# Eight reordered steps in a one-core kernel of four graph and four feed-forward layers on Trainium2

## The chip, the cores and the metric

The kernel runs on one core of one Trainium2 chip. The metric is the device time of one launch in microseconds. Before the change it is 889.49 us (median of 3 runs, 886.07 to 890.65).

## The reference

384 nodes with 512 features pass through eight residual steps, a graph step and a feed-forward step in each of four layers. Each gets the layer-normalised x and adds its result to x:

```
x = x + _L0_gnn_ref(_layernorm(x), edge_index, ...)   # attention over 6144 edges, softmax over nodes, elu, norm
x = x + _L0_ffn_ref(_layernorm(x))                    # the "shifter", below
x = x + _L1_gnn_ref(_layernorm(x), edge_index, ...)   # three graph convolutions with relu and graph norm
x = x + _L1_ffn_ref(_layernorm(x), w_up, w_down)      # quantised linear pair
x = x + _L2_gnn_ref(_layernorm(x), edge_index, W, b)
x = x + _L2_ffn_ref(_layernorm(x), ...)               # six experts, top 1, gelu
x = x + _L3_gnn_ref(_layernorm(x), src, dst, deg, ...)# self and neighbour product, bias, norm
x = x + _L3_ffn_ref(_layernorm(x), ...)               # 64 experts, top 8 of 4 groups
```

The shifter reads flags and three one-hot digits out of its normalised input and adds two one-hot digits to it:

```
hot = x_bd > 0.5
lo, hi, sa = first16(64), first16(80), first16(96)     # first hot position of 16, else 0
val = lo + 16 * hi
shl, shr = (val << sa) & 255, val >> sa
res = shl if mark and is_shl, shr if mark and is_shr, else 0
out = x_bd with 2*active*one_hot(res & 15) added at 128:144 and 2*active*one_hot(res >> 4) at 144:160
```

The last step, for each token:

```
scores = sigmoid(x2 @ gate_w.T); s = scores + gate_b
# the 4 groups of 8 experts with the largest sum of their two best s; the 8 best s inside them
w = chosen scores / their sum * 2.5
y = sum over the 8 chosen experts e of w_e * (silu(x2 @ w1[e]) * (x2 @ w3[e])) @ w2[e]
```

## The kernel before

The 384 tokens are three tiles of 128 partitions (NT = 3), the features four chunks of 128 (KD = 4). Everything is written by hand for five queues: SP (all plain loads and stores), GpSimd (gathers and scatters by index), TensorE, ScalarE and VectorE. Each is one list of instructions, executed in order, and semaphores join them. On VectorE `go` issues an instruction that counts up one semaphore, `settle` waits for all of them, `one` does both; an instruction that reads another's result stands behind a `settle`.

A **norm** on VectorE (`layernorm`, `tile_root` and `tile_norm`) takes statistics of a tile, has ScalarE take the root (`row_root`), inverts it and writes the normalised tile. TensorE transposes it (`transposes`) and ScalarE copies the transposed tile out of PSUM (`copy_T`). ScalarE's order of roots and copies is written out.

**Layer 0.** Scores of the edges are scattered to a table in DRAM of 384 x 384 x 8. SP reads it back in three tiles of 1.5 MB (L315), VectorE finds each row's maximum in `row_max` by halving (L1326, L1328), subtracts it (L1333), TensorE transposes and multiplies. Meanwhile GpSimd quantises weights (L472 to L474).

**Shifter** (L1372 to L1431). VectorE normalises x into xn3 in full width, and releases GpSimd, which adds xn3 to x3 (L478). VectorE goes on with small instructions on xn3: three comparisons of 48 columns (L1376), a maximum, some 30 instructions on 3 to 9 columns, six one-hots (L1427). Then it waits for GpSimd's adds and adds 32 columns (L1430). The norm for layer 1 ("3") follows.

**L3 graph step** ("7" and "8" are the norms ahead of it and behind it). TensorE: transposes of tile 0, `own_part(0)`, transposes of tiles 1 and 2, the neighbour product over all tiles (L768), then own and neighbour parts, then the transposes of norm 8 and the router's logits. ScalarE: root and copy alternate for the tiles of norm 7; for each tile of norm 8 two roots and one copy.

**Router.** After the sigmoid VectorE ranks the groups, and per tile takes the eight best (L1627), their positions (L1628) and replaces them (L1629); two comparisons and casts give `picked`, TensorE counts it (L788, L790) and VectorE has each token's place in its expert (`place1`, L1637).

**Experts.** 64 experts with 64 slots each make 32 expert tiles of two; eight places for overfull experts make two more (NTILE = 34). Weights come in 1.5 MB pieces into NWB = 11 buffers, two for each tile; the load of expert e waits for the `down` product of the tile that used its buffer (L335). Tile 0's tokens are picked by a matmul with one-hots (`pick_first_tokens`, L816). For the others VectorE takes slot codes out of PSUM (`take_code` for tiles 1 and 2, `take_slots` later), and GpSimd gathers 128 token rows from `tok_tab` in DRAM (L492), which SP has stored (L350). The loop per tile i on TensorE: `transpose_tokens(i + 1)` (L824), `transpose_hidden(i - 1)`, `up(i)` (L835), `find_slots(i + 3)`, `down(i - 1)` (L855), `combine(i - 2)` (L863). `combine` multiplies a one-hot spread with the result in three bf16 parts: ScalarE writes the high part (L1068), VectorE what is left (L1681), ScalarE the middle part (L1070), VectorE the low part (L1683). After the loop VectorE adds the three banks to x3 (L1818) and SP stores.

## Time and profile before

| | us |
|---|---|
| median of 3 runs (lowest, highest) | 889.49 (886.07, 890.65) |
| profiled execution, its time | 888.59 |
| profiled execution, its span | 886.9 |
| busy: TensorE, VectorE, ScalarE, GpSimd | 640.7, 532.8, 277.4, 229.4 |
| mean granted TensorE clock | 0.831 |

The span is the time between first and last instruction on the chip; the metric adds what lies around it. Positions (start us) count from the span's start. Busy times of different engines overlap, and only a view that tells what each instruction waited for says which of them costs time.

### The profile page before, as it was taken

How to read it: one execution, taken by the hardware profiler on the slowest of the kernel's cores; microseconds unless marked ns; L12 is line 12 of the kernel's file. 1: busy time of each engine (PE TensorE's matmuls, PEld its weight loads, DVE VectorE, ACT ScalarE, POOL GpSimd, SP SyncE). 2: the span in 40 equal slices, each digit the busy share in tenths (PEclk: the TensorE clock that was granted, in tenths of full speed). 3: DMA queues.
4: the chain of work that ended last, by engine and by line, in shares of the span. 5: the costliest groups of instructions: out<-in, count | busy, mean ns of one | idle time of the engine just before them, and what ended most of it. 6: DMA issues, size and time to landing. Idle time of an engine off the chain costs nothing.

```text
span 886.9 us, 9573 instructions
## 1 busy us (share of the span) xinstructions
PE 640.7 (72%) x2855; PEld 311.0 (35%) x2878; DVE 532.8 (60%) x1472; ACT 277.4 (31%) x1103; POOL 229.4 (26%) x232
## 2 busy tenths in 40 slices
PE   5952424433234850998588998848999999999997
PEld 3420112111112750445335554433344344344332
DVE  3457988679697979444635225664447844445533
ACT  2104755456563330333504011111222222222222
POOL 5154776676772721000000000001011011111100
PEclk9985556665555965999598999969999999999999
DMA  8599486776875707900300000285999999999991
GB/s 337 229 384 320 132 260 214 237 245 190 276 211 202 249 1 257 383 1 8 135 0 1 0 1 0 80 326 203 405 418 412 406 395 408 419 408 417 417 364 38
DMA packets 46502, 208.08 MB, mean 235 GB/s; under 512 B 7953, under 2 KB 12561, under 8 KB 36848
## 3 DMA queue, kind: packets, MB, share of 16 engines
q1 hardware_dynamic: 27152, 145.70, 41.5%
q0 software_dynamic: 19296, 61.75, 20.9%
q8 instruction: 24, 0.39, 0.2%
q14 instruction: 30, 0.25, 0.1%
HBM read 199.67 MB, written 10.31 MB: 237 GB/s over the span
## 4 chain that ended last, share of the span: by engine, by line
PE 48%; DVE 6%; DMA 4%; ACT 1%; issue 1%; DVEq 0%; POOLq 0%; SPq 0%
PE bank L835 11%; PE bank L863 6%; PE bank L855 6%; PE bank L725 4%; PE bank L740 3%; DMA R<-tok_tab,slot_tok 3%; PE bank L646 3%; PE bank L539 2%; PE bank L640 2%; PE bank L824 2%; PE bank L534 1%; PE bank L747 1%; DMA R<-L_w 1%; PE bank L695 1%; PE bank L768 1%
## 5 line engine op out<-in xcount | busy, mean ns | idle before, releaser
L583 PE MATMUL bank<-R 128*128 128x384 bf16 x144 | 50.0, 483 | 141.1 <-DVE R L1258 106.7
L960 ACT ACTIVATE R<-R 128x128 f32<-128x128 f32 x384 | 113.3, 296 | 103.2 <-DVE R L1297 73.6
L835 PE MATMUL bank<-R 128*64 128x512 f32 (+1 forms) x432 | 106.6, 602 | 0.5 <-ACT R L1050 0.5
L492 POOL DMA_INDIRECT R<-tok_tab,slot_tok x33 | 33.2, 1006 | 269.6 <-DVE slot_f L1657 212.2
L539 PE MATMUL bank<-R,late 128*128 128x512 f32 x168 | 79.8, 635 | 0.0
L960 ACT ACTIVATION_READ_ACCUMULATOR R<-R 128x1 f32 x384 | 72.1, 188 | 14.7 <-issue 14.6
L583 PEld LDWEIGHTS bank<-R 128*128 128x128 bf16 x144 | 13.3, 119 | 173.1 <-DVE R L1258 125.5
L863 PE MATMUL bank<-R 128*128 128x512 bf16 x284 | 68.5, 380 | 3.6 <-issue 1.9
L1669 DVE TENSOR_TENSOR R<-R,bank 128x256 f32<-128x256 f32 x34 | 14.3, 420 | 90.9 <-ACT R L1062 90.9
L1293 DVE TENSOR_TENSOR R<-R 128x1032 f32<-128x1032 f32 x48 | 59.0, 1229 | 15.8 <-DMA R<-tab_dst,e_i 12.0
L450 POOL DMA_INDIRECT score<-late,e_i x48 | 57.4, 1196 | 42.4 <-DVE late L1252 25.4
L436 POOL DMA_INDIRECT R<-tab_src,e_i x48 | 50.5, 1053 | 39.2 <-DMA tab_src<-R 24.1
L1297 DVE SCALAR_TENSOR_TENSOR R<-R,sm 128x1024 f32<-128x1024 f32 x48 | 59.0, 1228 | 1.7
L855 PE MATMUL bank<-R 128*64 128x512 f32 (+1 forms) x216 | 55.5, 599 | 0.5 <-ACT R L1056 0.5
L443 POOL DMA_INDIRECT R<-tab_dst,e_i x48 | 49.3, 1028 | 22.2 <-issue 13.7
L481 POOL MEMSET R<- 128x512 f32 x3 | 1.6, 526 | 201.0 <-DVEq L1584 200.9
L534 PE MATMUL bank<-ident,late 128*128 128x128 f32 x72 | 15.0, 375 | 49.0 <-DVE late L1176 35.2
L539 PEld LDWEIGHTS bank<-R,late 128*128 128x128 f32 x168 | 34.9, 210 | 42.3 <-issue 41.8
L835 PEld LDWEIGHTS bank<-R 128*64 128x64 f32 (+1 forms) x432 | 30.3, 134 | 48.2 <-issue 47.7
L863 PEld LDWEIGHTS bank<-R 128*128 128x128 bf16 x306 | 27.2, 98 | 56.4 <-DVE R L1675 23.6
L1062 ACT ACTIVATE R<-bank 128x256 f32<-128x256 f32 x34 | 13.1, 385 | 107.9 <-PE bank L835 107.9
L835 PE MATMUL bank<-late,R 128*64 128x512 f32 (+1 forms) x144 | 43.8, 598 | 0.0
(371 smaller groups left out, 1163.4 us busy)
## 6 DMA issues: line engine op xcount, KB each, us to landing
R<-L_w SPq DMA_DIRECT2D x54, 1536.0 KB, 10.7
late<-L_w SPq DMA_DIRECT2D x18, 1536.0 KB, 9.6
R<-L_w SPq DMA_DIRECT2D x2, 3072.0 KB, 15.2
score<-R POOLq DMA_DIRECT2D x9, 512.0 KB, 11.8
R<-score SPq DMA_DIRECT2D x3, 1536.0 KB, 10.1
R<-L_Ww SPq DMA_DIRECT2D x2, 2048.0 KB, 12.5
R<-L_W SPq DMA_DIRECT2D x4, 1024.0 KB, 9.0
tab_src<-R SPq DMA_DIRECT2D x3, 516.0 KB, 3.0
```

What stands on the lines that cost most here:

```text
L436: pool.indirect_dma_start(out=ga[j], out_offset=None, in_=tab_src[:, :], in_offset=bass.IndirectOffsetOnAxis(ap=src_i[:, t:t + 1], axis=0) ...
L443: pool.indirect_dma_start(out=gd[j], out_offset=None, in_=tab_dst[:, :], in_offset=bass.IndirectOffsetOnAxis(ap=dst_i[:, t:t + 1], axis=0) ...
L450: pool.indirect_dma_start(out=score[:, :], out_offset=bass.IndirectOffsetOnAxis(ap=row_i[:, t:t + 1], axis=0), in_=w_e3[:, t, :], in_offse ...
L539: last = pe.matmul(pb[bank][:, cols_], lhsT[:, k, P * t:P * t + P], rhs[:, k, :], start=(k == chunks_[0]), stop=(k == chunks_[-1]))
L583: last = pe.matmul(pb[s][:, 0:N], oh[:, e % 2, 0, P * s:P * s + P], oh[:, e % 2, 1, :], start=(e == 0), stop=(e == ET - 1))
L725: last = pe.matmul(pb[j % 3][:, 0:N], F2W1[:, e, k, P * c:P * c + P], xT[:, k, :], start=(k == 0), stop=(k == KD - 1))
L835: last = pe.matmul(pb[4 + i % 2][part, :], xeT[i % 2][:, k, part], w13[e % NWB][:, k, :], start=(k == 0), stop=(k == KD - 1), tile_positio ...
L855: last = pe.matmul(pb[7][part, :], hT[i % 2][:, c, part], w2e[e % NWB][:, c, :], start=(c == 0), stop=(c == 1), tile_position=(0, part.start))
L863: last = pe.matmul(pb[t][:, :], spread[i % NSM][:, P * t:P * t + P], y_part[i % 2][c], start=(i == 0 and c == 0), stop=(i == NTILE - 1 and ...
L960: act_.activation(own, own, ACT.Copy, accum_out=w_e3[:, t, h:h + 1]).then_inc(S("heads_summed"), 1)
L1293: tt(ga[j], ga[j], gd[t % NGD], ALU.add).then_inc(S("rows_added"), 1)
L1297: stt(prod[t % 2].rearrange(heads, h=H), ga[j][:, 0:2 * D].rearrange(heads, h=H), 0.0, bc(waR[:, None, :], [P, H, P]), ALU.max, ALU.mult). ...
```

## The change

1. SP reads the first score tile back in two halves (by node column), and `row_max(0)` takes the maximum over the first half when it has landed and the second when all has. The order of the comparisons differs, the result doesn't.
2. SP stores the three token tiles ahead of the loads of experts 5, 6, 7 and 9, each as soon as it is normalised.
3. GpSimd no longer adds xn3 to x3. ScalarE writes x3 · (1 + rstd) − mean · rstd in place instead, from two small vectors that VectorE makes. The norm ahead of the shifter writes columns 0 to 111 only, and the shifter is rewritten in fewer instructions.
4. TensorE runs `up(1)` ahead of the transposes of tile 2's tokens and of tile 0's hidden rows; the later tiles keep their order.
5. ScalarE takes the roots of tiles 1 and 2 of norm 7 ahead of the copy of tile 1, and the first root of tile 1 ahead of the copy of tile 0 in norm 8.
6. Router: the three maxima, then the three replacements, then `picked` at once in bf16; the searches for positions move behind the weight split; the copy of the loads moves behind the one-hots of tile 2.
7. `take_code(1)` stands ahead of `onehots(2)`.
8. The last expert tile is combined part by part (high, middle, low), and VectorE adds each bank when its last product is done.

```diff
@@ SP
-            for i in range(NT):
+            own = score[0:N * P, :].rearrange("(p n) h -> p n h", p=P)
+            sp.dma_start(mt[0][:, 0:N // 2], own[:, 0:N // 2]).then_inc(S("half_back"), 16)
+            sp.dma_start(mt[0][:, N // 2:N], own[:, N // 2:N]).then_inc(S("read_back0"), 16)
+            for i in range(1, NT):
...
             load_expert(8)
+            for t in range(NT):
+                sp.wait_ge(S("xn_ready"), nth("8", t + 1))
+                own = tok_tab[0:2 * P, :].rearrange("(p c) d -> p c d", c=2)[:, 0, :] if t == 0 else tok_tab[P + P * t:2 * P + P * t, :]
+                sp.dma_start(own, xn3[:, t]).then_inc(S("tokens_stored"), 16)
             sp.wait_ge(S("x_ready"), NT * 7)
             for e in (5, 6, 7, 9):
                 load_expert(e)
-            for t in range(NT):
...
@@ GpSimd
-            pool.wait_ge(S("shifter_in_ready"), 1)
-            for t in range(NT):
-                pool.tensor_tensor(out=x3[:, t, :], in0=x3[:, t, :], in1=xn3[:, t, :], op=ALU.add).then_inc(S("shifter_added"), 1)
@@ TensorE
+            def combine_last():
+                i = NTILE - 1
+                pe.wait_ge(S("spread_ready"), NTILE)
+                for c, part in enumerate(("y_high_ready", "y_mid_ready", "y_low_ready")):
+                    pe.wait_ge(S(part), NTILE)
+                    for t in range(NT):
+                        last = pe.matmul(pb[t][:, :], spread[i % NSM][:, P * t:P * t + P], y_part[i % 2][c], start=False, stop=(c == 2), skip_group_check=True)
+                        if c == 2:
+                            last.then_inc(S("combined"), 1)
...
-            for i in range(1, NTILE + 2):
+            for i in range(1, NTILE + 1):
+                if i == 1:
+                    up(1)
                 if i + 1 < NTILE:
                     transpose_tokens(i + 1)
                 if 1 <= i <= NTILE:
                     transpose_hidden(i - 1)
-                if i < NTILE:
+                if 1 < i < NTILE:
                     up(i)
...
+            combine_last()
@@ ScalarE
+            act_.wait_ge(S("shifter_in_ready"), 1)
+            for t in range(NT):
+                act_.activation(x3[:, t, :], x3[:, t, :], ACT.Identity, scale=V_("rstd_1", 3)[:, t:t + 1], bias=V_("nmr", 3)[:, t:t + 1]).then_inc(S("shifter_added"), 1)
...
+            row_root(0)
+            copy_T("7", 0)
+            row_root(1)
+            row_root(2)
+            copy_T("7", 1)
+            copy_T("7", 2)
+            row_root(0)
+            row_root(0)
+            row_root(1)
+            copy_T("8", 0)
+            row_root(1)
+            copy_T("8", 1)
+            row_root(2)
+            row_root(2)
+            copy_T("8", 2)
@@ VectorE, row_max
+                if i == 0:
+                    dve.wait_ge(S("half_back"), 16)
+                    go(tt(half_max[:, 0:768], mtf[i][:, 0:768], mtf[i][:, 768:1536], ALU.max))
+                    dve.wait_ge(S("read_back0"), 16)
+                    one(tt(half_max[:, 768:1536], mtf[i][:, 1536:2304], mtf[i][:, 2304:3072], ALU.max))
@@ VectorE, shifter
+            layernorm(x3, xn3, produce=add_norm(yr), produced=x_tile_ready(0), part=slice(0, 112))
+            go(stt(first, xn3[:, :, 64:112], 0.5, bc(fall48[:, None, :], [P, NT, 48]), ALU.is_gt, ALU.mult))
+            go(ts(mark, xn3[:, :, 0], 0.5, None, ALU.is_gt))
+            go(ts(flags[:, :, 1:3], xn3[:, :, 39:41], 0.5, None, ALU.is_gt))
+            go(ts(V_("rstd_1", 3), rstd, 1.0, None, ALU.add))
+            settle()
+            go(dve.tensor_reduce(far, V_("first", 144).rearrange("p (c i) -> p c i", i=16), AX, ALU.max))
+            stt(V_("nmr", 3), mv[:, :, 0], -1.0, rstd, ALU.mult, ALU.mult).then_inc(S("shifter_in_ready"), 1)
+            go(tt(both, shl, shr, ALU.mult))
+            settle()
...
+            one(tt(ones2, bc(iota64[:, None, None, 0:16], [P, NT, 2, 16]), bc(nibs[:, :, :, None], [P, NT, 2, 16]), ALU.is_equal))
+            go(tt(first[:, :, 0:32], first[:, :, 0:32], bc(amp[:, :, None], [P, NT, 32]), ALU.mult))
             settle()
             dve.wait_ge(S("shifter_added"), NT)
@@ VectorE, router
-                v8 = top8[:, 8 * t:8 * t + 8]
-                one(dve.max(v8, masked[:, t, :]))
-                go(dve.max_index(smi[:, 8 * t:8 * t + 8], v8, masked[:, t, :]))
-                go(dve.match_replace(replaced[:, t, :], v8, masked[:, t, :], NEG))
-            settle()
-            go(dve.tensor_copy(idx8f, smi[:, 0:24]))
+                go(dve.max(top8[:, 8 * t:8 * t + 8], masked[:, t, :]))
+            settle()
+            for t in range(NT):
+                go(dve.match_replace(replaced[:, t, :], top8[:, 8 * t:8 * t + 8], masked[:, t, :], NEG))
+            settle()
+            ts(WK[:, 1536:1632].bitcast(bf16), WK[:, 896:1088], -2e38, None, ALU.is_lt).then_inc(S("picked_ready"), 1)
             go(ts(WK[:, 1088:1280], WK[:, 896:1088], -2e38, None, ALU.is_lt))
-            settle()
-            dve.tensor_copy(WK[:, 1536:1632].bitcast(bf16), WK[:, 1088:1280]).then_inc(S("picked_ready"), 1)
...
-            dve.tensor_copy(load_s[:, :], pb[7][:, E3 * NT:E3 * NT + E3]).then_inc(S("place_used"), 1)
-            dve.wait_ge(S("place_used"), 1)
...
+            take_code(1)
             onehots(2)
-            take_code(1)
+            dve.tensor_copy(load_s[:, :], pb[7][:, E3 * NT:E3 * NT + E3]).then_inc(S("place_used"), 1)
+            dve.wait_ge(S("place_used"), 1)
@@ VectorE, end
-            dve.wait_ge(S("combined"), NTILE)
             for t in range(NT):
+                dve.wait_ge(S("combined"), NTILE + t)
                 tt(x3[:, t, :], x3[:, t, :], pb[t][:, :], ALU.add).then_inc(S("x_ready"), 1)
```

## Rows read from the trace of the kernel before

**Rows 1.** The page's chain that ended last, shares by engine:

```profile
PE 48%; DVE 6%; DMA 4%; ACT 1%; issue 1%; DVEq 0%; POOLq 0%; SPq 0%
```

**Rows 2.** Stretches: length, busy by engine, granted clock, DMA share, GB/s:

```profile
606.00:608.00 2.00, 2.00 (x8) 0.89 (x8) 1.33 (x7) 0.38 (x1) 1.01 (x1) 0.50 0.00 0
632.00:880.00 248.00, 243.47 (x1375) 96.28 (x1391) 127.06 (x450) 63.75 (x122) 27.00 (x27) 1.00 0.93 382
```

**Rows 3.** Landings of L315; timeline (start, length, engine, line, [idle before]):

```profile
DMA to landing us min/median/max: 6.7/10.1/13.3
...
284.82 1.76 DVE L1326 TENSOR_TENSOR R<-R 128x1536 f32<-128x1536 f32 x1 [2.48 <-DMA R<-score]
```

**Rows 4.** Timeline of the shifter; ScalarE's scaled Identity of the next layer:

```profile
339.52 1.13 DVE L1176 TENSOR_SCALAR late<-x_s,sm 128x512 f32<-128x512 f32 x2
340.69 2.64 DVE L1376 SCALAR_TENSOR_TENSOR sm<-late,fall 128x48 f32<-128x48 f32 x3
340.78 3.70 POOL L478 TENSOR_TENSOR x_s<-x_s,late 128x512 f32<-128x512 f32 x3 [25.51 <-DVEq L1373]
...
343.70 0.81 DVE L1380 TENSOR_SCALAR sm<-sm 128x9 f32<-128x9 f32 x1
...
345.04 0.16 DVE L1391 TENSOR_SCALAR sm<-late 128x3 f32<-128x3 f32 x1
...
349.41 0.26 DVE L1430 TENSOR_TENSOR x_s<-x_s,sm 128x96 f32<-128x96 f32 x1
...
422.28 0.81 ACT L1000 ACTIVATE late<-late,sm 128x512 f32<-128x512 f32 x1 [0.61 <-DVE sm L1473]
```

**Rows 5.** Timeline of the L3 graph step, VectorE and TensorE:

```profile
544.43 0.17 DVE L1196 RECIPROCAL sm<-sm 128x1 f32<-128x1 f32 x1 [2.40 <-ACT sm L934]
...
545.23 0.66 PE L534 MATMUL bank<-ident,late 128*128 128x128 f32 x4 [1.63 <-DVE late L1197]
...
568.55 0.16 DVE L1597 RECIPROCAL sm<-sm 128x1 f32<-128x1 f32 x1 [0.37 <-ACT sm L934]
```

**Rows 6.** Timeline of the router, VectorE, and the pick on TensorE:

```profile
585.49 0.23 DVE L1627 MAX8 sm<-R 128x8 f32<-128x64 f32 x1
...
587.95 0.26 DVE L1634 CAST R<-R 128x192 bf16<-128x192 f32 x1
...
589.36 0.23 DVE L1639 COPY load_s<-bank 128x64 f32<-128x64 f32 x1
...
591.62 4.34 PE L816 MATMUL bank<-R,late 128*128 128x128 f32 x24 [0.64 <-DVE R L1734]
```

**Rows 7.** Timeline of stores, gathers, token transposes; landings of all 33 gathers:

```profile
577.08 1.52 SPq L350 DMA_DIRECT2D tok_tab<-late  x3
...
597.26 1.12 POOL L492 DMA_INDIRECT R<-tok_tab,slot_tok  x1 [50.21 <-DVE slot_f L1729]
...
603.71 0.66 PE L824 MATMUL bank<-ident,R 128*128 128x128 f32 x4 [3.15 <-DMA R<-tok_tab,slot_tok]
...
621.50 0.66 PE L824 MATMUL bank<-ident,R 128*128 128x128 f32 x4 [0.29 <-DMA R<-tok_tab,slot_tok]
...
628.03 1.00 POOL L492 DMA_INDIRECT R<-tok_tab,slot_tok  x1 [7.64 <-DVE slot_f L1657]
...
637.80 0.60 PE L824 MATMUL bank<-ident,R 128*128 128x128 f32 x4
...
DMA to landing us min/median/max: 4.3/8.1/9.7
```

**Rows 8.** Chain (start, length, what) of the last load; timeline of the end:

```profile
856.97 8.07 DMA R<-L_w
...
867.19 3.57 PE bank L835 x32
...
877.08 2.12 PE L863 MATMUL bank<-R 128*128 128x512 bf16 x9
...
882.36 1.88 DVE L1818 TENSOR_TENSOR x_s<-x_s,bank 128x512 f32<-128x512 f32 x3 [2.29 <-PE bank L863]
```

94 lines of the change are left out of this document (40 added, 54 removed).

## The prediction

> **What bounds the kernel now.** I read four views in this order: the chain that ended last, the engine shares by stretch, the timelines of the edited stretches, and the landings of DMAs. The chain gives 48% of the span to TensorE, 6% to VectorE and 4% to DMA [rows 1]: no engine binds throughout, and each edit must be priced in its own stretch. In the expert loop (632 to 880) TensorE works 243.5 of 248 us at the full clock while the DMA share is 0.93 [rows 2]; so a saving ahead of the loop moves it as a whole, and nothing in it gets shorter. From 606 to 608 the granted clock is 0.50, the lower of its two levels (1.2 against 2.4 GHz) [rows 2], just behind a wait of TensorE for gathered tokens. In the stretches ahead of the loop the chain runs through VectorE (softmax, shifter, router) or passes back and forth between it and TensorE, and there a saved wait is a saved microsecond.
>
> All positions below are those of the profiled execution of before: its time is 888.59 us, its span 886.9, so 1.7 us lie around the span and stay. Its median is 889.49.
>
> **1. First read of the scores in halves.** VectorE waits 2.48 us for the read, then takes 1.76 us for the first maximum over 1536 columns [rows 3]. The three equal reads land 6.7, 10.1 and 13.3 us after issue, so one of them flows for some 3.6 us, and its first half lands 1.8 us ahead of the whole, at about 283.0, when VectorE has been free since 282.3. Half of 1.76 is 0.88; it runs in the wait, and the path keeps 0.9 us after the whole has landed. Gain 1.76 − 0.9 = 0.85, less the second issue on SP (0.33 to 0.43, mostly under the flow): **0.8**, bounds 0.3 and 0.9. The reads behind it come 0.4 later, and the second isn't wanted before the first has been worked on for some 9 us, 5 us after it lands. VectorE has no gap from here to 316, so all of it carries on.
>
> **2. Shifter and short norm.** The last normalised tile ends at 340.65, and the shifter's last add (349.41 + 0.26) lets the next norm begin at 349.71 [rows 4]. Of these 9.06 us, 2.64 go to three comparisons of 48 columns at 0.93 each and 0.81 to one instruction on nine columns; both lie inside GpSimd's three adds (340.78 to 344.48). Later instructions of that size take 0.16. After the change the adds are on ScalarE. The new VectorE chain has 16 links. Rows give 0.16 for a tiny instruction, 0.07 for each one behind it in its link, 0.04 to settle, 0.26 for 96 columns, so about 0.30 for 144 [rows 4]: 0.56 + 0.49 (comparison, then maximum) + 0.27 + 0.34 + 5 × 0.27 + 2 × 0.20 + 2 × 0.27 + 0.29 + 0.30 + 0.30 = 4.84, against 9.06: 4.2 less. ScalarE starts about 1.0 us into it; the nearest row is the scaled Identity in place on 128x512, 0.81 [rows 4], so three take 2.4 and end 1.4 us ahead of the VectorE chain. They are hidden; with a table load of 1.28 they still would be, and that same row shows Identity behind Sqrt without one. The norm with 112 columns in place of 512: 0.53 and 1.13 become three of about 0.2, and the end is then set by ScalarE's last root: 1.1 us earlier. Together 5.3, taken as **5.2**, bounds 3.8 (links at 0.30) and 5.6. What comes next: TensorE waits for norm 3, whose layer-1 weights are issued at 337.3 and wanted at 355.3; 5.2 sooner still leaves 12.8 us for transfers of the 9.0 us kind.
>
> The Trainium skill ("SBUF — State Buffer", "Who interferes with whom") says that a VectorE instruction with two SBUF inputs and a GpSimd instruction that reads SBUF block each other fully; the trace agrees with 0.93 us beside the adds where 96 columns later take 0.26.
>
> **3. L3 order on ScalarE.** The root of tile 2 stands behind the copy of transposed tile 1, which waits for TensorE; VectorE waits 2.40 and TensorE then 1.63 us for the last transposes, with the neighbour product behind them [rows 5]. With both roots ahead of that copy, tile 2 is normalised at 543.0, TensorE goes from 543.6 straight on: **1.6**. The copy is wanted only 10 us later. In the second norm VectorE waits 0.37 for a root behind a copy [rows 5]; that goes, and TensorE's product for the next tile is then due about 0.1 short of it: **0.3**. Bounds for both 1.2 and 2.1. The third tile's order has no wait to lose.
>
> **4. Router chain.** From the first MAX8 at 585.49 to TensorE at 588.27 each of three tiles runs maximum, index search and replacement in 0.66, then casts (the last at 587.95) [rows 6]. Now: three maxima 0.51, three replacements 0.62, one comparison that writes bf16 0.25, settling 0.1: 1.5 against 2.73, so 1.25 less. The copy of the loads (0.23 and its settling, 0.26) leaves the path between place and one-hots as well. Together **1.5**: one-hots at 588.1, the pick of tile 0's tokens at 590.1, its end 594.4 (4.34 as today [rows 6]), first up product 595.1 to 598.6, slots of tiles 0 to 2 done at 599.05. The index searches (3 × 0.22 + 0.25, about 0.9) now stand before the copy of the first one-hots at 598.1: it lands around 598.0 in the new order, 0.6 ahead of TensorE. Cover gone, they would cost 0.9.
>
> **5. Token stores and second tile.** Today the three stores are issued behind four expert loads of 1.5 MB; the first gather starts at 597.26 and TensorE stands 3.15 us until 603.71 [rows 7]. On SP the stores now come first, at 565.9, 571.5 and 577.1; the four loads slip from 574.8 to 577.6 and end near 596, wanted from 608 on. The gather then waits for the codes, which moved ahead of the second one-hots: 590.2, plus 0.8 from release to DMA as today, so 591.0. It now flies beside the loads. Today's, with one load beside it, took 6.4 us (597.26 to 603.7); of all 33 the median is 8.1 and the longest 9.7 [rows 7]; I take 8.1, since the loads run to 596: 599.1, just as TensorE is free. So the transposes of tile 1 move from 603.71 to 599.1, 4.6 earlier. Then up(1) waits only for the copy of these transposes (0.7), starts at 600.6 instead of 606.75, and takes 3.6 at full clock or 4.36 as today. Its cost: the hidden transposes of tile 0 now come right before its down product, whose copy on ScalarE (0.38) is no longer covered: +0.5. down(0) ends at 607.3 to 608.1 (today 612.9), tile 4's transposes come one period of 8.1 later, at 615.4 to 616.2, or at 615.6 by their gather (607.5 + 8.1), against 621.50 today with its wait of 0.29 [rows 7]. Gain from the router's start to here 5.3 to 5.9, which includes the 1.5 of part 4; I take **5.4**. Lower bound 3.0: gather at 9.7 (−1.6) and a further late one (−0.8). Behind it SP's stream of 61 loads starts with down(0), so it moves with the loop.
>
> The skill's "SBUF — State Buffer" ("SBUF: two separate sides") speaks against this part: a DMA issued by GpSimd can't get its descriptors written while VectorE copies in a two-port mode, and it gives 3.1 us in place of 0.62. The first gather would now be issued in the middle of VectorE's one-hots and copies. The trace disagrees so far: beside the weight splits the two first issues took at most 1.12 us against 1.00 [rows 7]. By the rule the sum would be 2.5 us longer, 876.2.
>
> **6. Last combine in parts.** Today nine products wait for the last low part, which ends at 880.1, and VectorE waits 2.29 us for them before its three adds, 1.88 [rows 8]. Nine take 2.12 [rows 8], so 0.21 each and 0.4 for a single one. Now the first three run once the high part is there, at 879.2 behind combine(32), three more up to 880.5 at the latest, and of the last three the first is complete at about 880.75, with adds starting per tile as they run (0.6 apart). First add 880.75 instead of 882.36: **1.6**. Bounds 1.0 (VectorE's own branch after its last split could hold it) and 1.7. Last store and its landing stay.
>
> **Sum.** 0.8 + 5.2 + 1.6 + 0.3 + 5.4 + 1.6 = 14.9; 888.6 − 14.9 = **873.7 us**. All lower bounds: 0.3 + 3.8 + 1.2 + 3.0 + 1.0 = 9.3, so 879.3; all upper: 0.9 + 5.6 + 2.1 + 5.9 + 1.7 = 16.2, so 872.4. The two other runs of before lie 2.5 below and 2.1 above this execution, and I leave that much outside.
>
> **Rivals.** (a) The DMA stream takes over at the end. The last expert load lands at 865.05 [rows 8], and the product that needs it starts at 867.2: only 2.1 us of air. If the first gather or the early loads hold the stream's start while TensorE gains, what exceeds 2.1 is lost: of part 5's 5.4 about 3 remain, 876.1. For it: DMA share 0.93 over the loop. Against: the stream is released by the same down(0) that I move. (b) Blocked descriptors or slower gathers at the start: 876 to 878, by part 5's lower bound. (c) Slower than before: each tile's gather has only 9.8 − 8.1 = 1.7 us of air (issue 628.03, transposes 637.80 [rows 7]). If the denser start left the queue so full that gathers took over 10.3 us, every one of some 28 tiles would wait 0.5 us or more, which eats the 14.9; at 10.5 us, 0.7 × 28 − 14.9 = 5 us slower, 893. Against: of 33 gathers none takes over 9.7, and the median in a loop with a full queue is 8.1 [rows 7]. (d) The shifter shrinks less, since VectorE's 0.93 is its own and not GpSimd's: the one comparison of 144 columns then keeps up to 1.8 of the 2.64 and the nine columns 0.6, 876.1.
>
> **Chances.** Forecast (871.5 to 876) 0.60; (a), (b), (d) together, or several parts at their lower bounds (876 to 880), 0.22; better than summed (868.5 to 871.5) 0.10; nothing or little of it visible (880 to 893.9) 0.05; (c) 0.03. Range 869.5 to 880, which takes in the low ends and one run-to-run step below. A measurement of this kernel can tell 0.5%, 4.4 us, from no change. Over 0.5% faster 0.94, within 0.03, slower 0.03.
>
> **What would show it.** First maximum split with its first half inside the wait; from the last normalised tile to the next statistics 4.8 us, no instruction on nine columns over 0.3; no wait of VectorE for a root at 544; TensorE's counts 1.25 us sooner after the first MAX8; first gather issued before the pick ends, with TensorE waiting under 1 us for it, and a clock that doesn't fall to 0.5 behind it; the loop's period still 8.12; the last add 1.6 us nearer to the last split. A wait for a gather in every tile, or one for the last expert load, would make the prediction wrong.

## The result and the profile after

| | before | after |
|---|---|---|
| median of 4 runs, us | 887.78 | 876.93 |
| lowest, highest | 885.52, 890.65 | 867.93, 880.2 |
| profiled execution, its time | 888.59 | 867.93 |
| profiled execution, its span | 886.9 | 866.1 |
| busy: TensorE, VectorE, ScalarE, GpSimd | 640.7, 532.8, 277.4, 229.4 | 638.3, 527.4, 278.5, 227.4 |

The ratio after to before is 0.986, 95% interval 0.9816 to 0.9905: 12.4 us less, between 8 and 16. The forecast was 873.7 with a range of 869.5 to 880. Two things must be kept apart from the start. The profiled execution of after is the fastest of its four runs, 20.7 us below the profiled one of before, and only some 13 of these belong to the change; and the sum of the forecast was 14.9, so it was also a little too high. Both are taken apart below.

After, the page's chain by engine (against [rows 1]):

```profile
PE 58%; DVE 21%; issue 8%; ACT 6%; DMA 4%; POOL 2%; another core or an unknown queue 1%; DVEq 0%; SPq 0%; POOLq 0%
```

The two lines can't be compared: the shares of before add up to 60%, because its chain is followed back only to 348.5 us, near the end of the shifter, while that of after reaches back to the start. So the 48% and 6% from which the prediction started say nothing on the softmax and next to nothing on the shifter. Its prices don't rest on them.

After, two stretches, with length, busy by engine, granted clock, DMA share, GB/s (against [rows 2]):

```profile
586.00:588.00 2.00, 2.00 (x10) 0.67 (x12) 1.48 (x11) 0.00 (x0) 0.64 (x1) 1.00 0.03 11
612.00:858.00 246.00, 242.31 (x1369) 95.72 (x1386) 125.77 (x449) 63.15 (x121) 26.95 (x27) 1.00 0.94 383
```

The second up product (586 to 588 lies in it) now runs at the full clock, where in before it ran at 0.50. The loop is as full as before, TensorE 242.3 of 246 us; nothing in it got shorter.

After, timelines (start, length, engine, line, [idle before]) of the first maximum and of norm and shifter (against [rows 3, 4]):

```profile
280.17 0.96 DVE L1351 TENSOR_TENSOR R<-R 128x768 f32<-128x768 f32 x1 [0.40 <-DMA R<-score]
282.06 0.96 DVE L1353 TENSOR_TENSOR R<-R 128x768 f32<-128x768 f32 x1 [0.93 <-DMA R<-score]
...
331.62 0.32 DVE L1200 TENSOR_SCALAR late<-x_s,sm 128x112 f32<-128x112 f32 x1
...
331.98 0.71 DVE L1200 TENSOR_SCALAR late<-x_s,sm 128x112 f32<-128x112 f32 x2
332.72 0.31 DVE L1407 SCALAR_TENSOR_TENSOR sm<-late,fall 128x144 f32<-128x144 f32 x1
...
333.69 2.22 ACT L987 ACTIVATE x_s<-x_s,sm 128x512 f32<-128x512 f32 x3 [2.05 <-DVE sm L1414]
...
337.31 0.26 DVE L1458 TENSOR_TENSOR x_s<-x_s,sm 128x96 f32<-128x96 f32 x1
```

The first half of the maximum runs in the wait for the second. ScalarE's three adds end at 335.91, 1.4 us ahead of the last add of VectorE, as reckoned. But a write of 112 columns takes 0.32, not 0.2.

After, timelines of the third layer's graph step, the router and the first tiles (against [rows 5 to 7]):

```profile
528.49 0.16 DVE L1220 RECIPROCAL sm<-sm 128x1 f32<-128x1 f32 x1 [0.34 <-ACT sm L947]
...
529.12 1.04 PE L534 MATMUL bank<-ident,late 128*128 128x128 f32 x8
...
570.05 0.48 DVE L1654 MAX8 sm<-R 128x8 f32<-128x64 f32 x3
...
571.59 0.23 PE L788 MATMUL bank<-R,trib 128*128 128x64 bf16 x1 [6.84 <-DVE R L1659]
...
575.59 1.12 POOL L492 DMA_INDIRECT R<-tok_tab,slot_tok  x1 [44.48 <-DVE slot_f L1753]
```

```profile
574.68 5.25 PE L816 MATMUL bank<-R,late 128*128 128x128 f32 x24 [0.64 <-DVE R L1758]
...
584.46 0.66 PE L824 MATMUL bank<-ident,R 128*128 128x128 f32 x4
...
585.90 3.65 PE L835 MATMUL bank<-R 128*64 128x512 f32 x16 [0.54 <-DVE R L1687]
...
590.92 0.27 PE L803 MATMUL bank<-tok_w,R 128*64 128x4 bf16 x6 [0.56 <-ACT R L1080]
...
601.10 0.60 PE L824 MATMUL bank<-ident,R 128*128 128x128 f32 x4
```

The waits of 2.40 and 1.63 us of the third layer are gone (0.34 is the plain path of a root). The counts come 1.54 us behind the first MAX8, where it was 2.78. The first gather is issued before the pick ends; TensorE takes its tokens at 584.46 with no wait, where it stood for 3.15 us. The price named beforehand is there too: 0.56 us behind the hidden transposes.

After, timeline of the end (against [rows 8]):

```profile
858.99 2.10 PE L864 MATMUL bank<-R 128*128 128x512 bf16 x9
...
860.85 1.88 DVE L1848 TENSOR_TENSOR x_s<-x_s,bank 128x512 f32<-128x512 f32 x3 [0.82 <-PE bank L864]
861.56 2.27 SPq L376 DMA_DIRECT2D out<-x_s  x3
```

The adds start 0.82 us after VectorE's last split, where it was 2.29. The last row was not expected: the issues of the three output stores stretch over 2.27 us.

**One view of all.** Stretches between fixed points, from the starts and lengths in the timelines of each profiled execution. "Others like before" are experiments in which the code of that stretch is that of before; the next column has three executions of the changed kernel (the second and third are experiments 1 and 9).

| stretch, us | before | others like before | after, three times |
|---|---|---|---|
| score read issued to first maximum's end | 8.52 | 8.29 to 8.72 | 7.52, 7.41, 7.42 |
| to the last scaled softmax tile | 40.62 | 36.87 to 40.64 | 36.86, 37.90, 36.85 |
| to the last write of the norm | 13.45 | 13.44, 13.45 | 12.81, 12.81, 12.81 |
| to the shifter's last add | 9.02 | 9.02, 9.03 | 4.88, 4.90, 4.88 |
| to layer 2's last graph add | 114.65 | 114.72 to 116.48 | 115.24, 116.17, 114.77 |
| layer 2: last graph add to gate logits | 11.49 | 11.47 to 11.69 | 9.14, 11.72, 11.50 |
| gate logits to layer 3's norm done | 69.49 | 69.48 to 69.49 | 67.42, 67.43, 67.42 |
| to the router's start | 35.35 | 35.35 | 35.85, 35.86, 35.84 |
| to the first MAX8 | 4.83 | 4.83, 4.84 | 4.83, 4.83, 4.83 |
| first MAX8 to the counts | 2.77 | 2.77 | 1.54, 1.54, 1.54 |
| counts to the transposes of the fourth tile | 33.23 | 33.29 to 33.83 | 29.50, 28.54, 29.74 |
| these to the last split | 258.57 | 257.44 to 258.95 | 258.92, 258.37, 257.60 |
| last split to the last add's end | 4.17 | 4.17 | 2.71, 2.71, 2.70 |
| last add's end to the span's end | 2.62 | 2.61, 2.62, 2.62 | 3.39, 3.86, 4.09 |

Seven of these stretches repeat to 0.02 us. The others don't: the first maximum, the softmax, the layers between shifter and layer 2, the middle of layer 2, the way to the fourth tile, the expert loop and the end of the changed kernel; nor do the 275 to 282 us ahead of the score read. In the profiled pair three of them fell the same way, 2.6 us before the score read, 3.8 in the softmax and 2.3 in layer 2, together 8.7, with nothing of the change in their code; 0.9 fell the other way (0.6 behind the shifter, 0.35 in the loop). The edited stretches make up the remaining 13.

**A stretch that may take something back.** From the shifter's last add to layer 2's last graph add no instruction was edited. It takes 114.65 to 114.81 in the four executions with GpSimd's adds (before, experiments 3, 5 and 6), and 114.54 to 116.48 in the nine with ScalarE's adds and no additional work ahead of norm 3 (all others but experiment 12), in the mean 0.9 more. More than half of that (0.55) is the first product behind norm 3, here in before:

```profile
355.28 10.65 PE L539 MATMUL bank<-R,late 128*128 128x512 f32 x24
```

In experiment 2 the same 24 instructions start at 346.82 and take 11.76. In before the granted clock is 1.00 from 356 on, 0.7 us behind the product's start; in experiment 2 it is still 0.50 from 347 to 349, up to 2.2 us behind it. Three of the nine are as short as before, so the earlier shifter doesn't lengthen the stretch every time. Whether it does so more often, or six of nine against none of four is chance, no run settles.

### The profile page after: what moved, and what is told of

Same layout as the page of the kernel before. It is cut to its first block, busy times and chain, and to the rows that moved or that the text cites. A ratio compares the mean times of both kernels' runs of the same rounds, so it can differ in the third digit from the quotient of the medians.

```text
span 866.1 us, 9566 instructions
## 1 busy us (share of the span) xinstructions
PE 638.3 (74%) x2855; PEld 309.7 (36%) x2878; DVE 527.4 (61%) x1465; ACT 278.5 (32%) x1106; POOL 227.4 (26%) x229
## 4 chain that ended last, share of the span: by engine, by line
PE 58%; DVE 21%; issue 8%; ACT 6%; DMA 4%; POOL 2%; another core or an unknown queue 1%; DVEq 0%; SPq 0%; POOLq 0%
PE bank L835 13%; PE bank L539 7%; PE bank L873 7%; PE bank L855 6%; ACT R L973 4%; PE bank L725 4%; PE bank L740 4%; DVE R L1317 3%; DVE R L1321 3%; PE bank L646 3%; PE bank L640 2%; PE bank L824 2%; PE bank L534 2%; PE bank L747 1%; PE bank L752 1%
## 5 line engine op out<-in xcount | busy, mean ns | idle before, releaser
L873 PE MATMUL bank<-R 128*128 128x512 bf16 x275 | 66.4, 380 | 2.6 <-issue 2.1
L835 PEld LDWEIGHTS bank<-R 128*64 128x64 f32 (+1 forms) x432 | 30.1, 133 | 47.9 <-issue 46.7
## 6 DMA issues: line engine op xcount, KB each, us to landing
R<-L_Ww SPq DMA_DIRECT2D x2, 2048.0 KB, 12.4
```

Of the source, the lines that this page charges most:

```text
L835: last = pe.matmul(pb[4 + i % 2][part, :], xeT[i % 2][:, k, part], w13[e % NWB][:, k, :], start=(k == 0), stop=(k == KD - 1), tile_positio ...
L873: last = pe.matmul(pb[t][:, :], spread[i % NSM][:, P * t:P * t + P], y_part[i % 2][c], start=(i == 0 and c == 0), stop=False, skip_group_c ...
```

## The experiments

The theory: the gains are local, each about as priced, they add up, and nothing behind them takes them back. The rivals are named in each expectation. "Part" is a part of the prediction (1 to 6), not a number of the list of changes. Experiments 1 to 4, 5 to 8, 9 to 11 and 12 ran on four chips, each group beside runs of before on its own chip, with medians of before of 887.71, 872.24, 874.56 and 886.2. So only ratios are compared across groups.

**1, 9. The changed kernel again**, with no edit.

> The changed kernel once more, nothing altered, to see which of the stretches of its first profiled execution belong to the change. Theory (the gains are local, as priced): the stretches that the change touches come out again within 0.3 us: last norm store to the shifter's last add about 4.9, score read's issue to the first maximum's end about 7.5, third router maximum to the third tile's transposition about 31, last split to the last add 2.7; those that it does not touch and that differed (last maxima to the softmax's end 35.0, against 38.8 before; second layer's middle 7.2, against 9.5 before; edge stage 275.5, against 278.1 before) may come out at either length, following TensorE's granted clock. Median near 876. Rival (the change itself moved the softmax and the second layer): these stretches are short again, 35 and 7.2, in this execution too, with the clock high in the last softmax tile, and before's are long again.

> The changed kernel a third time, as the measure for the next two on one chip, and as a third look at the stretches that vary. Theory: ratio to the kernel before 0.986 again; score read to first maximum 7.4 to 7.5, shifter 4.9, third layer's stretch 67.4, first MAX8 to the transposes of tile 3 30 to 31, last add to end 3.4 to 4.1. The softmax stretch (36.9 to 40.7 in ten executions of all kernels) and the second layer's middle (9.1 once, 11.5 to 11.7 else) follow TensorE's clock, not the kernel. Rival: the change's gain is smaller than 1.4% and the first two measurements were lucky: ratio 0.990 or more.

Measured: ratios 0.9864 (0.9815 to 0.9913; 876.49 us) and 0.9867 (0.9823 to 0.9911; 862.29 us). Three measurements agree, 0.986, 0.9864 and 0.9867: 1.36%, 12 us. The table shows the rest: the stretches that the change touches came out again, and softmax and layer 2 went back to longer values in one or both, so they aren't the change's.

**2. Part 2 alone.** Before, with ScalarE's adds, the short norm and the new chain:

```
-            pool.wait_ge(S("shifter_in_ready"), 1)
-            for t in range(NT):
-                pool.tensor_tensor(out=x3[:, t, :], in0=x3[:, t, :], in1=xn3[:, t, :], op=ALU.add)...
+            act_.wait_ge(S("shifter_in_ready"), 1)
+            for t in range(NT):
+                act_.activation(x3[:, t, :], x3[:, t, :], ACT.Identity, scale=V_("rstd_1", 3)[:, t:t + 1], ...
...
-            layernorm(x3, xn3, produce=add_norm(yr), produced=x_tile_ready(0))
+            layernorm(x3, xn3, produce=add_norm(yr), produced=x_tile_ready(0), part=slice(0, 112))
```

> The kernel before with part 2 of the change alone: ScalarE's adds in place of GpSimd's, the shorter write in the norm, the rewritten shifter. Theory (each gain is local and they add up): about 4.8 us less than the kernel before (shifter 9.06 to 4.9, norm 1.70 to 1.07), ratio 0.9945. Rival (an earlier start of what follows runs against a later wait or a lower clock): under 3 us, with the shifter's own stretch still at 4.9. Rival (the shifter's saving also frees the second layer's middle, since the stages after it meet a warmer TensorE): 7 us or more, second layer's middle at 7.2.

Measured: 0.9935 (0.9904 to 0.9966), 882.66 us, 5.1 less by medians. Norm 12.81, shifter 4.88, as in the changed kernel. Layer 2's middle is 11.69, so the second rival is out. The first isn't: the layers between took 116.48, 1.8 more than in before, and the medians' difference, 5.1 ± 2.8, fits 4.8 and also 3.

**3. The start of the expert loop alone.** Before, with the router's chain, the token stores ahead, the second up product ahead, `take_code(1)` ahead:

```
+            for t in range(NT):
+                sp.wait_ge(S("xn_ready"), nth("8", t + 1))
+                ...
+                sp.dma_start(own, xn3[:, t]).then_inc(S("tokens_stored"), 16)
             sp.wait_ge(S("x_ready"), NT * 7)
             for e in (5, 6, 7, 9):
                 load_expert(e)
...
+                if i == 1:
+                    up(1)
                 if i + 1 < NTILE:
                     transpose_tokens(i + 1)
```

> The kernel before with the router's shorter chain, the token stores ahead of the four weight loads, the second tile's expert ahead of the third tile's transpositions and the hot code taken earlier. Theory: third maximum to third tile's transposition falls from 36.0 to about 31, and the kernel by 5 us, ratio 0.9945. Rival (the loop's steady course gives part of it back, because the weights arrive later behind the token stores or the gathers stay late): the stretch falls by 5 but the kernel by under 3 us. Rival (the saving depends on the warm clock that the third-layer order brought): first tiles at a lower clock again, stretch at 33 to 34, kernel 2 to 3 us less.

Measured: 0.9926 (0.9895 to 0.9958), 880.87 us, 6.8 less by medians. First MAX8 to the fourth tile's transposes 30.99, where it was 36.01, without the third layer's new order. The 5 us arrive at the end: from there to the last split it takes 258.44, as before.

**4. Who held VectorE in the shifter?** Before, with GpSimd's three adds given to ScalarE; VectorE's old chain and the long norm stay:

```
-                pool.tensor_tensor(out=x3[:, t, :], in0=x3[:, t, :], in1=xn3[:, t, :], op=ALU.add)...
+                act_.activation(x3[:, t, :], x3[:, t, :], ACT.Identity, scale=V_("rstd_1", 3)[:, t:t + 1], ...
```

> The kernel before with only GpSimd's three shifter adds replaced by three of ScalarE; VectorE's old chain of the shifter, the long norm and the rest stay. It settles whether the first comparisons of the shifter (0.93 us each beside GpSimd's adds) were long by themselves. Theory (they were held up by GpSimd's adds, which run in the same time): the three comparisons and the reduction after them fall to about 0.2 to 0.35 us each, the shifter from 9.06 to 6.5 to 7.5 us, the kernel by about 2 us. Rival (VectorE's own time): the comparisons stay at 0.93 us each and the stretch at 8.5 or more.

Timeline of experiment 4 (against [rows 4]):

```profile
337.41 0.44 DVE L1377 SCALAR_TENSOR_TENSOR sm<-late,fall 128x48 f32<-128x48 f32 x3
337.53 2.22 ACT L971 ACTIVATE x_s<-x_s,sm 128x512 f32<-128x512 f32 x3 [2.10 <-DVE sm L1374]
...
338.22 0.17 DVE L1381 TENSOR_SCALAR sm<-sm 128x9 f32<-128x9 f32 x1
```

The same three comparisons take 0.44 where they took 2.64, the instruction on nine columns 0.17 where it took 0.81, and the shifter 6.45 where it took 9.02. So 2.57 of the 4.14 us come from the adds' change of engine, though it has two small instructions more in its chain (0.4), and 1.57 from the shorter chain. Rival (d) is out: the 0.93 us were GpSimd's. The time, 885.51 us, ratio 0.9988 (0.9956 to 1.0019), is compatible with 2.6 us and with nothing (here too the layers behind took 116.23).

**5. The other three parts.** Before, with the halves of the score read, the new order of the third layer and the last combine by parts:

```
-            for t in range(NT):
-                row_root(t)
-                copy_T("7", t)
+            row_root(0)
+            copy_T("7", 0)
+            row_root(1)
+            row_root(2)
+            copy_T("7", 1)
+            copy_T("7", 2)
...
+            sp.dma_start(mt[0][:, 0:N // 2], own[:, 0:N // 2]).then_inc(S("half_back"), 16)
+            sp.dma_start(mt[0][:, N // 2:N], own[:, N // 2:N]).then_inc(S("read_back0"), 16)
...
+            combine_last()
```

> The kernel before with the three parts that neither of the two part kernels had: the first score read in halves, the order of roots and copies of the third layer on ScalarE, the last combine by parts. Theory (local gains): score read's issue to the first maximum's end 8.6 to 7.5, the third layer's stretch up to the router 1.6 shorter, last split to last add 4.2 to 2.7, but up to 1.2 of the last given back behind the last add; together 2.9 to 4.0 us less than before, which with 5.8 and 6.6 us of the two other part kernels makes up the whole change's 12 only if these two medians are some 3 us too good. Rival (the three parts are worth nothing on the path, the two others make up the whole): under 1 us less, with these stretches as before. Rival (a further loss from the earlier start): slower than the sum by over 1 us, seen as a longer loop.

Measured: 0.9957 (0.9927 to 0.9986), 868.89 against 872.24 us, 3.4 less by medians. First maximum 7.36, layer 3's norm 67.42, last add's end 2.70 behind the last split, all as in the changed kernel, and the end 4.08 behind it. Experiments 2, 3 and 5 together are 1.8% (0.65, 0.74, 0.43, each ± 0.3), the whole change is 1.4 ± 0.3% by its three ratios: no contradiction, and no proof that they add to the tenth either. In the edited stretches the part kernels and the whole change have the same lengths.

**6. The last combine alone:**

```
+            def combine_last():
+                ...
+                for c, part in enumerate(("y_high_ready", "y_mid_ready", "y_low_ready")):
+                    pe.wait_ge(S(part), NTILE)
+                    for t in range(NT):
+                        last = pe.matmul(pb[t][:, :], spread[i % NSM][:, P * t:P * t + P], y_part[i % 2][c], ...
...
-            for i in range(1, NTILE + 2):
+            for i in range(1, NTILE + 1):
...
+            combine_last()
...
-            dve.wait_ge(S("combined"), NTILE)
             for t in range(NT):
+                dve.wait_ge(S("combined"), NTILE + t)
```

> The kernel before with the last combine by parts alone. Two executions of the changed kernel had 3.4 and 3.9 us from the last add's end to the end, all executions without this part 2.6, because the issue of the second output store took 1.2 and 1.7 us on SP in place of 0.34. Theory (the earlier stores run into the two instruction fetches that come a fixed time behind the last split): the second issue is again over 1 us here, last add to end 3.4 to 3.9, net gain of the part 0.3 to 0.7 us. Rival (it is the queue's position, moved by the additional score read): the issue is 0.34 here, last add to end 2.6, net gain 1.45 us.

SP's output stores: the timelines of before and of experiment 6 (start, from the first issue to the end of the last):

```profile
883.07 1.53 SPq L373 DMA_DIRECT2D out<-x_s  x3
```

```profile
867.17 2.79 SPq L373 DMA_DIRECT2D out<-x_s  x3
```

Measured: 1.0001 (0.9974 to 1.0027). The last add ends 1.47 us nearer to the last split, and the end comes 3.90 us behind it in place of 2.62: 1.3 of 1.5 us are given back. It is the trace that tells this; the ratio, ± 2.3 us, can't. The position of the stores on their queue isn't the cause, since the additional score read is absent here.

**10. Is it SP?** The changed kernel with the second store on ScalarE's queue:

```
-            for t in range(NT):
+            for t in (0, 2):
                 sp.wait_ge(S("x_ready"), NT * 7 + t + 1)
...
+            act_.wait_ge(S("x_ready"), NT * 7 + 2)
+            act_.dma_start(out[P:2 * P, :], x3[:, 1]).then_inc(S("half_back"), 16)
```

> The changed kernel with the second output store issued by ScalarE, which has long been idle, in place of SP. In five executions of kernels with the last combine by parts one of SP's three store issues took 1.2 to 1.7 us in place of 0.34, and last add to end 3.4 to 4.1 in place of 2.6. Theory (SP's own issue is held, by its queue or an instruction fetch): with only two stores on SP, and ScalarE's beside them, last add to end is 2.6 to 3.0, 0.8 to 1.2 us less than the changed kernel. Rival (the DMA engines or their rings are held, whoever issues): one of the issues is long again and the end comes 3.4 us or more behind the last add; no gain.

Measured: 0.9852 (0.9808 to 0.9896), not to be told from the changed kernel. Every issue is short or nearly so (0.35, 0.37 and 0.60), and still the end is 3.38 behind the last add. Experiment 9 has all three issues short and its end is the latest of all, 4.09. So no issue is long, as the rival's sign had it, but its core holds: a second issuing queue gains nothing, so the issuing queue isn't what is held. What the packets in the traces show, in us from the last add's end (the output's packets belong to q1, the 16 KB one to q8, which the page calls instruction):

```
                 16 KB instruction packet   last output packet ends   span's end
before                     -1.99                     1.89                2.62
experiment 2               -1.99                     1.88                2.61
experiment 3               -1.93                     1.89                2.62
after                      -0.66                     2.65                3.39
experiment 1               -0.67                     3.13                3.86
experiment 6               -0.64                     3.16                3.90
experiment 9               +0.03                     3.28                4.09
experiment 10              -0.68                     2.57                3.38
```

The fetch comes 2.0 to 2.7 us behind the last split in all of them. In before that is 0.8 us ahead of the first store; with the combine by parts the stores have come forward into it, and their packets all but stop, from 0.5 to 1.0 in after and to 1.5 us in experiments 1 and 6, or straggle one by one in experiment 9. That the two stand together in all eight is measured, and the other six executions agree: the end comes 2.61 or 2.62 behind the last add in the four without the combine by parts, 3.37 to 4.09 in the ten with it. In seven of these ten SP issues all three stores and the 16 KB packet starts 0.64 to 0.70 ahead of the last add's end. There a longer such packet goes with a later end of the output: 2.65 and 2.63 for 0.93 and 1.02 us, 2.92 and 2.93 for 1.21, 3.05 for 1.36, 3.13 and 3.16 for 1.41 and 1.43. That the fetch holds the packets is still inferred; no run took the fetch away.

**7. Token stores back behind the loads.** The changed kernel with

```
-            for t in range(NT):
-                ...
-                sp.dma_start(own, xn3[:, t]).then_inc(S("tokens_stored"), 16)
             sp.wait_ge(S("x_ready"), NT * 7)
             for e in (5, 6, 7, 9):
                 load_expert(e)
+            for t in range(NT):
+                ...
+                sp.dma_start(own, xn3[:, t]).then_inc(S("tokens_stored"), 16)
```

> The changed kernel with one part undone: the three token stores again behind the loads of four experts. Theory (the first gather waits for these stores, as before): the first gather is issued again some 11 to 12 us behind the first of the last three MAX8 in place of 5.5, the transposes of tile 1 come 18 us behind it in place of 14.4 with TensorE waiting 3 to 4 us and its clock at 0.5 after that, and the kernel is 3.5 to 4.5 us slower than the changed one (about 880.5). Rival (the codes set the first gather, the stores have long landed): under 0.5 us slower. Rival (the four loads gain by going first): faster than the changed kernel.

Timelines of experiment 7:

```profile
576.11 1.11 POOL L492 DMA_INDIRECT R<-tok_tab,slot_tok  x1 [50.28 <-DVE slot_f L1753]
```

```profile
582.29 1.10 PE L824 MATMUL bank<-ident,R 128*128 128x128 f32 x4 [2.78 <-DMA R<-tok_tab,slot_tok]
...
584.17 6.12 PE L835 MATMUL bank<-R 128*64 128x512 f32 x16 [0.53 <-DVE R L1687]
```

The first gather is issued 11.3 us behind the first MAX8 (564.78) in place of 5.5, TensorE waits 2.78, and its clock falls: the second up product takes 6.12 where it takes 3.65. First MAX8 to the fourth tile 37.2, against 30.1 to 31.3: 6 to 7 us in this execution, and longer even than before's 36.0 to 36.6. The time says less: 865.78 us, 0.9909 (0.9877 to 0.9941), against 0.9864 for the changed kernel (mean of its three ratios), 3.9 us slower with some 4 either way.

**8. Second up product back.** The changed kernel with

```
-                if i == 1:
-                    up(1)
...
-                if 1 < i < NTILE:
+                if i < NTILE:
                     up(i)
```

> The changed kernel with one part undone: the up product of tile 1 again behind the transposes of tile 2 and the hidden ones of tile 0. Theory: the transposes of tile 2 must wait for the second gather, which comes some 2 to 4 us behind the first, so TensorE stands before them, the up product starts 2 to 4 us later, the transposes of tile 4 come at 32 to 34 us behind the first MAX8 in place of 30 to 31, and the kernel is 1.5 to 3 us slower. Rival (the second gather is there at once): the order is worth only what the hidden transposes' wait costs, the stretch is 29.5 to 30.5, so the old order would be as good or 0.5 us better.

Timeline of experiment 8:

```profile
578.28 0.71 PE L824 MATMUL bank<-ident,R 128*128 128x128 f32 x4 [1.45 <-DMA R<-tok_tab,slot_tok]
578.78 0.63 PE L844 MATMUL bank<-ident,R 128*128 128x128 f32 x2
579.34 5.03 PE L835 MATMUL bank<-R 128*64 128x512 f32 x16
```

TensorE waits 1.45 for the second gather, then runs the up product partly cold (5.03), and the fourth tile comes 33.8 behind the first MAX8, 2.6 to 3.8 later than in the changed kernel, as the theory said. The time, 0.9858 (0.9807 to 0.9908) from four runs, doesn't show it; its interval of ± 4.4 us can't.

**11. Does the clock make the two varying stretches?** The changed kernel with work that nobody reads, in TensorE's waits:

```
+            def keep_warm(n):
+                for _ in range(n):
+                    pe.transpose(pb[7][:, 0:P], ident[:, :], ident[:, :])
...
+                    if i == NT - 1 and c == 0:
+                        pe.wait_ge(S("half_sc_ready"), 1)
+                        keep_warm(10)
                     transpose_scores(i, c)
...
+            keep_warm(26)
             for t in range(NT):
                 if t == 0:
                     pe.wait_ge(S("x_ready"), NT * 4 + NT)
```

> The changed kernel with 36 additional transposes of the identity into a bank that nobody reads: 10 ahead of the last softmax tile's transpositions, 26 in the 3.9 us in which TensorE waits for the second layer's norm. Nothing else changes. Theory (the two stretches are long where TensorE's clock has fallen in the wait ahead of them): the second layer's middle falls from 11.5 to about 9.2, the softmax stretch stays at 36.9 to 38, with no 40.6 to 40.7, and the kernel is 2 to 4 us faster than the changed one. Rival (the clock falls all the same, since its level was decided before these stretches): the middle stays at 11.5 or more, the kernel is the same or up to 1 us slower by the additional work.

Layer 2's middle without the additional work (experiment 9), then with it (experiment 11):

```profile
445.45 2.79 PE L534 MATMUL bank<-ident,late 128*128 128x128 f32 x12 [3.88 <-DVE late L1200]
448.18 3.88 PE L708 MATMUL bank<-late,wg_s 128*6 128x128 f32 x24
```

```profile
442.97 3.00 PE L622 MATMUL bank<-ident 128*128 128x128 f32 x26
447.02 1.54 PE L534 MATMUL bank<-ident,late 128*128 128x128 f32 x12 [1.04 <-DVE late L1208]
448.48 2.79 PE L716 MATMUL bank<-late,wg_s 128*6 128x128 f32 x24
```

And the granted clock there (windows; the clock is the third number from the end), experiment 9, then 11:

```profile
446.00:450.00 4.00, 4.00 (x20) 2.99 (x19) 3.44 (x12) 2.06 (x6) 0.00 (x0) 0.50 0.00 0
```

```profile
447.00:451.00 4.00, 3.98 (x36) 3.27 (x36) 3.88 (x13) 2.12 (x6) 0.00 (x0) 1.00 0.02 4
```

At 0.50 (1.2 GHz), reached in the wait of 3.88 us, the twelve transposes take 2.79; at 1.00 (2.4 GHz), held with 3 us of additional work in that wait, 1.54. The wait alone doesn't decide it: in the profiled execution of after, TensorE waits the same 3.88 us with no additional work, the clock stays at 1.00, and the transposes take 1.54. Measured: 855.6 us, ratio 0.9775 (0.9733 to 0.9816), against 0.9867 for the changed kernel on the same chip. That is faster than both kernels. The stretch fell from 11.50 to 9.14. That explains 2.4 of the 6.7 us between the two medians; the profiled softmax, 36.85 in both, explains nothing, and the rest is within the intervals.

**12. More of it:** experiment 11 with 57 more transposes, 30 ahead of norm 3's, 22 during the router's grouping, 5 behind the counts.

```
+            pe.wait_ge(S("shifter_in_ready"), 1)
+            keep_warm(30)
...
+            pe.wait_ge(S("sigmoid_ready"), 1)
+            keep_warm(22, 6)
             pe.wait_ge(S("picked_ready"), 1)
...
+            keep_warm(5, 6)
```

> The kernel with the 36 additional transposes, and 57 more: 30 in the wait ahead of norm 3's transposes (from the shifter's input on), 22 while VectorE works on the router's groups, 5 behind the counts. Theory (stretches that begin cold behind a long wait of TensorE can be warmed in that wait): the first transposes of norm 3 take 1.5 us in place of 2.8, the product behind them starts at the full clock, so that the graph layers' stretch is 1.5 to 2.5 us shorter than its 69.4; the pick of tile 0's tokens falls from 5.3 to 3 to 4.5 us, of which at most 1 us reaches the transposes of tile 3, since the first gather comes then. Ratio to the kernel before 0.973 to 0.976. Rival (the clock falls again soon behind the additional work, or has not risen when it ends): these stretches as before, ratio 0.9775 to 0.979. Rival (the additional work itself gets in the way, being cold it takes 0.22 to 0.24 each): slower than 0.9775 with TensorE still in it when its inputs are ready.

Timeline of experiment 12:

```profile
339.11 5.98 PE L622 MATMUL bank<-ident 128*128 128x128 f32 x30 [16.20 <-DVE sm L1427]
345.97 1.63 PE L534 MATMUL bank<-ident,late 128*128 128x128 f32 x12 [0.88 <-DVE late L1213]
...
578.00 5.40 PE L828 MATMUL bank<-R,late 128*128 128x128 f32 x24 [0.64 <-DVE R L1771]
```

Measured: 869.89 us, 0.9804 (0.978 to 0.9828). Norm 3's transposes took 1.63 us and the graph layers 68.1 in place of 69.3 to 70.5; layer 2's middle was 9.14 again. The pick stayed cold, 5.40, with 27 transposes ahead of it: the clock was 1.00 from 574 to 576 and had fallen again before the pick began at 578. There the first rival holds. And the softmax was 40.73 long although its last tile ran at the full clock: this time the tile before it was cold, so the ten transposes ahead of the last tile are no cure. The ratio missed the 0.973 to 0.976 that the theory named; experiments 11 and 12 can't be told apart by their ratios.

## Why the prediction held, and where it didn't

The result is faster, as forecast, and inside the range, but not in the part of it that was given 0.60 (871.5 to 876). The median of after, 876.93, lies in the next one (876 to 880, 0.22), which was meant for rivals (a), (b) and (d) or several parts at their lower bounds. None of these came; what lacks is mostly part 6. Mean of the three executions of after against the mean of all like before, part by part:

| part | predicted | measured | how it came |
|---|---|---|---|
| 1 halves | 0.8 (0.3 to 0.9) | 1.1 (8.56 to 7.45) | right, above the bound |
| 2 shifter | 4.2 | 4.1 | right, its split too (experiment 4) |
| 2 short norm | 1.1 | 0.64 | mechanism right, mis-sized |
| 3 layer 3's order | 1.9 (1.2 to 2.1) | 1.6 (2.07 − 0.50) | right, a third term missing |
| 4, 5 router to fourth tile | 5.4 (3.0 to 5.9) | 5.5 (1.23 + 4.22) | right |
| 6 last combine | 1.6 (1.0 to 1.7) | 0.3 (1.47 − 1.16) | step "last store and its landing stay" wrong |
| sum (part 2 was taken as 5.2) | 14.9 | 13.2 | |

The measured sum fits the measured ratios, 12.1 us ± 2.3. With the unedited layers behind the shifter, 0.7 us longer in these three executions than in the four with GpSimd's adds, it would be 12.5; whether that belongs to the change is open, as said above.

**Part 1.** Of its 1.1, 0.80 is the shorter instruction behind the landing (1.76 to 0.96), as reckoned. The rest is that the second half is worked on 6.6 us after the first issue (282.06 − 275.49), where the whole was in before 6.8 and, in four other executions, between 0.2 sooner and 0.2 later; I had reckoned 0.1 of loss there.

**Part 2.** The term that was mis-sized is the row for 112 columns: "about 0.2" each, against 0.32 alone and 0.71 for two. So the last write is behind ScalarE's last root by its own length and the stretch gains 0.64. The shifter is 4.88 against 4.84 reckoned. By the Trainium skill ("SBUF — State Buffer", "Who interferes with whom") a VectorE instruction with two SBUF inputs and a GpSimd instruction that reads SBUF shut each other out for a whole instruction; experiment 4 agrees, 2.64 to 0.44 us for the three comparisons, which have two. The instruction on nine columns has one input and still fell from 0.81 to 0.17; the same section of the Trainium skill counts scalings like it among those that can take the shared ports in a two-port mode.

**Part 3.** The wait at 544 went and brought 1.85: the norm is done 2.07 sooner, and the product behind it starts 0.22 further behind, because the transposes of two tiles now run ahead of it (529.12, 1.04 for 0.66). The second wait of 0.37 went, a wait of 0.21 for TensorE's product came, and 0.2 is left of the 0.3. What no step had is a third term: the last transposes ahead of the router now fall on the lower clock. The timelines of before, then of after:

```profile
576.91 0.63 PE L534 MATMUL bank<-ident,late 128*128 128x128 f32 x4 [2.60 <-DVE late L1197]
```

```profile
561.01 1.09 PE L534 MATMUL bank<-ident,late 128*128 128x128 f32 x4 [2.42 <-DVE late L1221]
```

That is 0.46 of loss, 1.6 in all, and it isn't chance: the stretch from the first neighbour product's scaling to the router is 32.80 in every execution with the old order and 33.07 to 33.09 in every one with the new.

**Parts 4 and 5** are the core of the forecast. The first gather was put 5.5 us behind the first MAX8 (591.0 − 585.49) and came at 5.54; TensorE doesn't wait for it, the clock is 1.00 at the second up product, the hidden transposes cost 0.56 (0.5). That the sum came out to 0.1 is in part luck. The gather landed 5.1 us behind its issue (4.6 in experiments 1 and 9), where 8.1 had been taken; this gained nothing, since TensorE was busy for 3.8 us more (3.3 and 4.5). The pick was cold, 5.25 and 5.49 for 4.34 in two of the three executions (4.27 in the third). Against that stand the second up product at the full clock (3.65, where the sum allowed for 4.36) and before's stretch from the counts to the fourth tile, 33.5 over five executions, 0.3 above the profiled one. By the traces of experiments 7 and 8 both moves are needed, since either undone leaves TensorE in a wait for a gather with a fallen clock behind it; the time of experiment 8 doesn't show it. The rule of the Trainium skill that spoke against this part ("SBUF — State Buffer", "SBUF: two separate sides": descriptors of GpSimd's DMAs wait for VectorE's two-port copies) cost nothing here: the first gather's issue is 1.12 us, as before, and its tokens are there in time. But it was hardly put to the test: beside that issue (575.59 to 576.71) VectorE had one copy, of 64 columns out of PSUM, and beside the second one (581.21, 1.03 us) one cast of 192 columns. Rivals (a), (b) and (c) are out with it: from the fourth tile to the last split it takes 257.6 to 258.9 us with the change and 257.4 to 258.95 without, and the median of the gathers' landings is 8.1 again.

**Part 6.** The step that failed is its last sentence. The first add came when it was to come (0.82 behind the last split, 0.7 reckoned), but what lies behind the last add doesn't "stay": it was 2.62 with the stores just behind an instruction fetch, and it is 3.4 to 4.1 with the stores moved into it (that the fetch is the cause is inferred, as said there). A trace of experiment 6 alone would have told: 0.2 us of gain in place of 1.6.

**The base.** The sum was made against 888.59, the profiled run; 13.2 off the median of 887.78 is 874.6, and the median of after, 876.93, is 2.3 above, within its interval.

## What to carry to other kernels

Compare stretches, not totals: stretches that an edit doesn't touch and that differ in a pair of profiles are chance until they repeat, and here they were 8.7 of 20.7 us. Price an edit at the very end together with the transfers behind it, since what was short because of its place is not short in another. Where TensorE stands for some microseconds ahead of work that others wait for, look at the granted clock behind the wait; a few useless transposes in the wait can be worth more than a shorter chain, though of the four waits tried here they helped in two (layer 2 and norm 3).

## What the runs showed that was not expected

- With the combine by parts the output stores coincide with an instruction fetch of 16 KB that comes 2.0 to 2.7 us after the last split, and last add to end is 0.8 to 1.5 us longer in ten executions of ten, with a second issuing queue too. The cause is inferred.
- The layers behind the shifter, which nobody edited, took 114.5 to 116.5 us, the longer values only in kernels with the new shifter adds (six of nine against none of four); open.
- The granted clock takes its own course: the same softmax code took 36.85 to 40.73 us in 14 executions, depending on which tile the 0.50 fell on, and layer 2's middle 9.14 in two of twelve executions without additional work and 11.47 to 11.72 in the other ten.
- The chips differ by 1.8%: medians of before of 872.24 and 887.71 us. The difference lies ahead of the score read, which was issued at 259.4 to 266.4 us on two chips and at 277.0 to 281.7 on the two others; behind it no stretch goes with the chip. Each chip ran one group only.
- An instruction with one input of nine columns was held by GpSimd's adds too: 0.81 us beside them, 0.17 without.
- The third layer's new order puts the last transposes on the lower clock (1.09 for 0.63) each time, nine executions of nine, though it only removes waits ahead of them.
